# The ramp of a graph attention stage reordered

## The reference

```
h   = layernorm(x)                                  # [N, 256]
s1  = (h @ W[:256]) @ a_w ;  s2 = (h @ W[256:]) @ a_w
e   = s1[:, None] + s2[None, :] + a_b
e   = where(e >= 0, e, 0.2 * e) ;  e = where(adj > 0, e, -9e15)
x   = x + softmax(e, axis=1) @ (h @ fc_w + fc_b)
```

## Time and profile before

| | |
|---|---|
| median of the runs | 1169.57 us |
| profiled execution, its span | 1167.08 us, 1165.3 us |
| TensorE busy | 1032.5 us, 89% |
| VectorE busy | 757.0 us, 65% |
| ScalarE busy | 618.3 us, 53% |
| mean granted TensorE clock | 0.949 |
| first product of the ramp | 16.32 us |
| first exponential | 67.09 us |

### The profile page before, as it was taken

How to read it: one execution, slowest core, us unless ns; L and a number is a source line. 1 busy time by engine, 2 the same in 40 slices (tenths; PEclk the granted TensorE clock), 3 DMA queues, 4 the chain that set the end, 5 groups by cost and what they waited for, 6 DMA issues and landing times. The chain is left out here.

```text
span 1165.3 us, 23845 instructions
## 1 busy us (share of the span) xinstructions
PE 1032.5 (89%) x7616; PEld 823.2 (71%) x7617; DVE 757.0 (65%) x1598; ACT 618.3 (53%) x948; POOL 446.8 (38%) x363
## 2 busy tenths in 40 slices
PE   6639999999999599898987999996499999999991
PEld 5538989898989589687754888885266666666661
DVE  3799999999992464855675566666355455454550
ACT  1677888888873577767642112221145454454441
POOL 0244666666662000019140134453134444444443
PEclk9969999999999599899999999998699999999996
DMA  9998777777710311220053799998323333333322
GB/s 379 191 299 270 228 248 230 245 229 244 235 50 1 112 73 63 83 73 1 1 118 81 187 246 225 256 245 298 117 46 46 54 51 48 54 46 54 51 40 23
DMA packets 72587, 161.49 MB, mean 139 GB/s; under 512 B 7504, under 2 KB 58448, under 8 KB 66512
## 3 DMA queue, kind: packets, MB, share of 16 engines
q1 hardware_dynamic: 48656, 97.59, 26.9%
q0 software_dynamic: 18128, 40.17, 19.6%
q10 hardware_dynamic: 5744, 22.94, 5.5%
HBM read 137.34 MB, written 45.49 MB: 157 GB/s over the span
## 5 line engine op out<-in xcount | busy, mean ns | idle before, releaser
L554 PE MATMUL PS<-G,PT 128*128 128x256 f16 x2028 | 233.6, 273 | 0.0
L554 PEld LDWEIGHTS PS<-G,PT 128*128 128x128 f16 x2028 | 198.4, 98 | 22.1
L1576 PE MATMUL PS<-W,X 128*128 x708 | 165.5, 384 | 8.6 <-DVE X L1732 6.6
L1576 PEld LDWEIGHTS PS<-W,X 128*128 128x128 f16 x708 | 69.5, 98 | 97.0 <-issue 31.7
L1502 PE MATMUL PS<-own_H,adj_room 128*128 128x256 f16 x572 | 129.3, 272 | 0.0
L1500 PE MATMUL PS<-own_H,adj_room 128*128 128x257 f16 x572 | 129.3, 273 | 0.0
L1822 POOL DMA_INDIRECT out_dram<-X,place_i x59 | 92.2, 1563 | 88.4 <-DVE place_i L1746 80.6
L420 DVE SCALAR_TENSOR_TENSOR score<-S2low,S1low,S2row 128x3327 f32<-128x3327 f32 x26 | 114.5, 4405 | 1.4 <-ACT S2low L299 1.4
L538 PE MATMUL PS<-ident,probs 128*128 128x128 f32 x676 | 90.5, 280 | 26.0 <-ACT probs L327 16.8
L1596 PE MATMUL PS<-adj_room,X 128*128 x472 | 111.6, 380 | 0.3 <-issue 0.3
L426 DVE CUSTOM_DVE_ANT_0 score<-score,maskbias 128x3327 f32<-128x3327 f32 x26 | 100.0, 3848 | 6.2 <-DVE score L420 6.0
(11 more groups left out here) (273 smaller groups left out, 1991.8 us busy)
## 6 DMA issues: line engine op xcount, KB each, us to landing
adjf<-adj_dram SPq DMA_DIRECT2D x26, 1664.0 KB, 8.0
slot_rows<-blank SPq DMA_DIRECT2D x26, 1032.0 KB, 10.9
adj_room<-adjT_dram POOLq DMA_DIRECT2D x22, 832.0 KB, 9.8
W<-eW_dram ACTq DMA_DIRECT2D x8, 1024.0 KB, 4.8
adj_room<-eW_dram ACTq DMA_DIRECT2D x8, 1024.0 KB, 9.1
X<-slot_rows SPq DMA_DIRECT2D x59, 129.0 KB, 3.3
own_H<-eb_dram SPq DMA_DIRECT2D x8, 512.0 KB, 5.2
adj_room<-eW_dram ACTq DMA_DIRECT2D x8, 512.0 KB, 7.5
```

The lines of the kernel that those rows point to most:

```text
L554: mm = nc.tensor.matmul(acc[u][:, 0:D], left, right, start=(j == 0 and n == 0), stop=(j == T - 1 and n == 2))
L1576: mm = nc.tensor.matmul(psHE[u][:, n * F1:(n + 1) * F1], left[u][:, k, :], W1[:, e, k, part, n * F1:(n + 1) * F1], start=(m == 0), stop=(m ...
```

## The change

- **u on VectorE.** W is loaded as it stands (four blocks of 128 rows by 256), aw as a row that all 128 partitions hold. Four multiply-and-sum operations give uw [128, 4]. fcw moves from ScalarE's queue to the head of SP's.
- **Centring beside it.** The column sums of fcw and of u are made apart, by TensorE from fcw and from uw directly; the copies into fcwx are gone, and VectorE writes the centred result there. All of this stands ahead of row_moments(0) now.
- **Moments one group ahead.** row_moments(1) and gains(0) come before group 0; gains(n+1) and row_moments(n+2) stand inside group n, after the G_lo of its first pair. ScalarE's deviation(n+1) comes ahead of group n's G_hi.
- **Row copies two tiles earlier, mask of tile 0 earlier.** row_back(c) stands after G_hi(4c+5), not G_hi(4c+7); no_edge(0) stands ahead of the G_hi of the last group.
- **First score row in two parts.** leaky and masked of tile 0 for columns 0 to 2559 stand before the last four G_lo, those for the rest after them; a maximum of two joins them.

```diff
-        WT = score[1][:, 0:KD * 2 * D].rearrange("p (k n) -> p k n", k=KD)
+        W = score[1][:, 0:2 * KD * D].rearrange("p (k n) -> p k n", k=2 * KD)
...
         @block.sync
+            sp.dma_start(fcw[:, :, :], dram["fcw"].rearrange("(k p) n -> p k n", p=P)).then_inc(fcw_in, 16)
...
         @block.scalar
-            act.dma_start(WT[:, :, :], dram["WT"].rearrange("(k p) n -> p k n", p=P)).then_inc(u_in, 16)
-            act.dma_start(aw[:, :], dram["aw"]).then_inc(u_in, 16)
-            act.dma_start(fcw[:, :, :], dram["fcw"].rearrange("(k p) n -> p k n", p=P)).then_inc(fcw_in, 16)
+            act.dma_start(aw, dram["aw"]).then_inc(u_in, 16)
+            act.dma_start(W[:, :, :], dram["W"].rearrange("(k p) n -> p k n", p=P)).then_inc(u_in, 16)
...
-            deviation(0)
             act.wait_ge(fcw_in, 16)
             nc.scalar.activation(probs[0][:, 0:KD * D], fcw[:, :, :].rearrange("p k d -> p (k d)"), ACT.Square,
                                  accum_out=fsq[:, :]).then_inc(f_squared, 1)
+            deviation(0)
...
             for n, (a, b) in enumerate(XG):
-                if n > 0:
-                    deviation(n)
-                if n == len(XG) - 1:
+                if n + 1 < len(XG):
+                    deviation(n + 1)
+                else:
                     nc.scalar.activation(spent[:, :], big[:, :], ACT.Exp, scale=-1.0).then_inc(exp_waits, 1)
+                    no_edge(0, 0)
                 for i in range(a, b):
                     G_hi(i)
-                    if i % 4 == 3 and i >= 7:
-                        row_back((i - 7) // 4)
-            for c in range((T - 8) // 4 + 1, len(CK)):
-                row_back(c)
-            no_edge(0, 0)
+                    if i % 4 == 1 and i >= 5:
+                        row_back((i - 5) // 4)
+            row_back(len(CK) - 1)
             no_edge(1, 1)
...
         @block.vector
+            def leaky_part(n, a, b):
+                dve.wait_ge(s_low, 1)
+                dve.wait_ge(row_copied, 2 * -(-b // (4 * P)))
+                v.scalar_tensor_tensor(score[0][:, a:b], S2low[:, a:b], S1low[:, 0:1], S2row[:, a:b], ALU.add,
+                                       ALU.max).then_inc(leaky_part_done, 1)
+
+            def masked_part(n, a, b):
+                dve.wait_ge(mask_ready, 1)
+                dve.wait_ge(leaky_part_done, n + 1)
+                v.tensor_tensor_reduce(score[0][:, a:b], score[0][:, a:b], bias[0][:, a:b], 1.0, -2 * FAR,
+                                       ALU.subtract, ALU.max, part_max[:, n:n + 1]).then_inc(parts_done, 1)
...
+            dve.wait_ge(u_in, 32)
+            for m in range(2 * KD):
+                v.tensor_tensor_reduce(uj[m], W[:, m, :], aw, 1.0, 0.0, ALU.mult, ALU.add, uw[:, m:m + 1]).then_inc(u_done, 1)
+            dve.wait_ge(fcw_in, 16)
+            dve.wait_ge(mean_done, 1)
+            for k in range(KD):
+                v.scalar_tensor_tensor(fcwx[:, k, 0:D], psM[:, 0:D], -1.0 / D, fcw[:, k, :], ALU.mult,
+                                       ALU.add).then_inc(centred, 1)
+            dve.wait_ge(u_summed, 1)
+            v.tensor_scalar(u_mean[:, :], psU[:, 0:2], -1.0 / D, None, ALU.mult).then_inc(u_added, 1)
+            dve.wait_ge(u_added, 1)
+            for k in range(KD):
+                v.tensor_tensor(fcwx[:, k, D:D + 2], uw[:, k:k + 3:2], u_mean[:, :], ALU.add).then_inc(centred, 1)
             row_moments(0)
...
+            row_moments(1)
+            gains(0)
+            early = CK[-2][0] * P
             for n, (a, b) in enumerate(XG):
-                if n > 0:
-                    row_moments(n)
-                gains(n)
                 row_scores(a // 2)
                 for q in range(a // 2, b // 2):
                     if 2 * q + 2 < b:
                         row_scores(q + 1)
+                    if 2 * q + 4 == T:
+                        leaky_part(0, 0, early)
+                        masked_part(0, 0, early)
                     G_lo(2 * q)
                     G_lo(2 * q + 1)
+                    if 2 * q == a:
+                        if n == 0:
+                            dve.wait_ge(s_ready, 2)
+                            v.tensor_scalar(S1low[:, 0:4], S12[:, 0:4, 0], ALPHA - 1.0, None, ALU.mult).then_inc(s_low, 1)
+                        if n + 1 < len(XG):
+                            gains(n + 1)
+                        if n + 2 < len(XG):
+                            row_moments(n + 2)
...
-            leaky(0, 0)
-            masked(0, 0)
+            leaky_part(1, early, N)
+            masked_part(1, early, N)
+            dve.wait_ge(parts_done, 2)
+            v.tensor_tensor(rowmax[0][:, :], part_max[:, 0:1], part_max[:, 1:2], ALU.max).then_inc(masked_ready, 1)
             leaky(1, 1)
             masked(1, 1)
...
         @block.tensor
-            pe.wait_ge(u_in, 32)
-            for m in range(2 * KD):
-                for k in range(KD):
-                    mm = nc.tensor.matmul(psU[:, m:m + 1], WT[:, k, m * P:(m + 1) * P], aw[:, k:k + 1],
-                                          start=(k == 0), stop=(k == KD - 1))
-            mm.then_inc(u_done, 1)
             pe.wait_ge(unit_set, 1)
+            pe.wait_ge(fcw_in, 16)
+            for k in range(KD):
+                mm = nc.tensor.matmul(psM[:, 0:D], unit[:, :], fcw[:, k, :], start=(k == 0), stop=(k == KD - 1))
+            mm.then_inc(mean_done, 1)
+            pe.wait_ge(u_done, 2 * KD)
+            for k in range(KD):
+                mm = nc.tensor.matmul(psU[:, 0:2], unit[:, :], uw[:, k:k + 3:2], start=(k == 0), stop=(k == KD - 1))
+            mm.then_inc(u_summed, 1)
             pe.wait_ge(f_squared, 1)
```

More of the change, by code:

```diff
@@ L164, in attention @@
         xT = PT[:, :, :].rearrange("p q n -> p (q n)").bitcast(F32).rearrange("p (t k n) -> p t k n", t=T, k=KD)
-        WT = score[1][:, 0:KD * 2 * D].rearrange("p (k n) -> p k n", k=KD)
-        fcw = score[1][:, KD * 2 * D:KD * 3 * D].rearrange("p (k n) -> p k n", k=KD)
+        W = score[1][:, 0:2 * KD * D].rearrange("p (k n) -> p k n", k=2 * KD)
+        fcw = score[1][:, 2 * KD * D:3 * KD * D].rearrange("p (k n) -> p k n", k=KD)
+        aw = score[1][:, 3 * KD * D:3 * KD * D + D]
+        uj = [score[1][:, (3 * KD + 1 + m) * D:(3 * KD + 2 + m) * D] for m in range(2 * KD)]
         raw = sb("raw", [P, 8 * P])
@@ L169, in attention @@
         unit = raw[:, 8 * P - P:8 * P]
-        aw = sb("aw", [P, KD])
+        uw, u_mean = sb("uw", [P, 2 * KD]), sb("u_mean", [P, 2])
         ab, ab_low = sb("ab", [P, 1]), sb("ab_low", [P, 1])
@@ L176, in attention @@
         S1low = sb("S1low", [P, T])
-        big, spent = sb("big", [P, 1]), sb("spent", [P, 1])
+        big, spent, part_max = sb("big", [P, 1]), sb("spent", [P, 1]), sb("part_max", [P, 2])
         small = lambda n: [sb(f"{n}{u}", [P, 1]) for u in range(2)]
@@ L462, in iteration @@
                     leaky(t + 3, 1 - u)
-            row_moments(0)
-            dve.wait_ge(fcw_in, 16)
-            for k in range(KD):
-                v.tensor_copy(fcwx[:, k, 0:D], fcw[:, k, :]).then_inc(u_copied, 1)
-            dve.wait_ge(u_done, 1)
-            for k in range(KD):
-                v.tensor_copy(fcwx[:, k, D:D + 2], psU[:, k:k + 3:2]).then_inc(u_copied, 1)
+            dve.wait_ge(u_in, 32)
[11 more added lines that the diff above has]
+                v.tensor_tensor(fcwx[:, k, D:D + 2], uw[:, k:k + 3:2], u_mean[:, :], ALU.add).then_inc(centred, 1)
+            row_moments(0)
             dve.wait_ge(f_rooted, 1)
@@ L477, in _ @@
             v.tensor_scalar(g_scale[:, :], frecip[:, :], FULL / ROW_BOUND, None, ALU.mult).then_inc(f_chain, 1)
-            dve.wait_ge(mean_done, 1)
-            for k in range(KD):
-                v.scalar_tensor_tensor(fcwx[:, k, :], psM[:, 0:D + 2], -1.0 / D, fcwx[:, k, :], ALU.mult,
-                                       ALU.add).then_inc(centred, 1)
             dve.wait_ge(ab_in, 16)
@@ L574, in iteration @@
                     products(t - 1, 1 - u, 3)
-            pe.wait_ge(u_in, 32)
-            for m in range(2 * KD):
-                for k in range(KD):
-                    mm = nc.tensor.matmul(psU[:, m:m + 1], WT[:, k, m * P:(m + 1) * P], aw[:, k:k + 1],
-                                          start=(k == 0), stop=(k == KD - 1))
-            mm.then_inc(u_done, 1)
-            pe.wait_ge(unit_set, 1)
+            pe.wait_ge(unit_set, 1)
+            pe.wait_ge(fcw_in, 16)
[6 more added lines that the diff above has]
+            mm.then_inc(u_summed, 1)
             pe.wait_ge(f_squared, 1)
             nc.tensor.matmul(psR[0][:, 0:1], unit[:, :], fsq[:, :], start=True, stop=True).then_inc(f_summed, 1)
-            pe.wait_ge(u_copied, 2 * KD)
-            for k in range(KD):
-                mm = nc.tensor.matmul(psM[:, 0:D + 2], unit[:, :], fcwx[:, k, :], start=(k == 0), stop=(k == KD - 1))
-            mm.then_inc(mean_done, 1)
             pe.wait_ge(ident_in, 16)
-            pe.wait_ge(centred, KD)
```

(5 more changed lines are left out.)

11 lines of the change are left out of this document (6 added, 5 removed).

## The result

The changed kernel took 1164.91 us, the median of seven runs between 1163.17 and 1166.14. The kernel before, run beside it, took 1171.04 (seven runs, 1167.49 to 1175.29). The ratio is 0.9952, with a 95% interval of 0.9935 to 0.997: 5.6 us faster, between 3.5 and 7.6. The time is inside the predicted range, but at its fast end, and what happened is the rival in which W comes early, not the forecast: the first sum on VectorE started at 8.6 us, not at 10.3. The profiled execution took 1166.08 us (span 1164.3, mean granted clock 0.95).

What follows compares the result with a forecast made beforehand. TensorE and VectorE are full in the loop, so only the ramp's length counts: 13.0 less W's landing 10.3 less clock 0.9 gives 1.8 us, 1169.57 to 1167.8 us; 8-in-10 range 1164.0 to 1172.5.

Steps and rivals of the forecast that it cites:

- the rival in which W comes early: Load queues: W lands under 9.5 us, gain 3.5 to 5.7, time 1164 to 1166 us; chance 0.23.
- the forecast: Ramp: w 9.5 to 13 with a clock price of 0 to 1.8, time 1166 to 1171 us; chance 0.50.
- W's landing: Load queues: ScalarE's and SP's packets alternate, W's 512 rows gain 190 beyond their turn, landed at 10.3 us; ends 7.3 and 15.
- The even share of bytes: Load queues: turns by whole packets of descriptors give W at 7.3 us, gain 5.7; chance 0.07, within early W's 0.23.
- From W to the end of the first row: Ramp from W's landing to the end of tile 0's first mask-and-max: 50.3 us, against 51.2 from fcw's landing before.
- w: Start of the ramp: the moment W and aw have landed, taken as 10.3 us.
- The clock: TensorE in the ramp: a stall may bring 1.2 GHz, costing 1.8 us; half taken, 0.9 us.
- The reordering itself is thus worth 0.9 us.: Ramp behind the landing: three us won in the tail, about as many lost to mask(0), two stalls replace three; 0.9 us.
- The loop: Attention loop behind the ramp: untouched, PE and DVE full, so all of the earlier start is passed on.
- Strict alternation: Load queues: w = 13.5 to 15, loss 0.5 to 2, with the clock up to 3.8, 1170 to 1173.4 us; chance 0.14.
- TensorE at 1.2 GHz through the middle: Ramp: clock low from w + 20 to w + 30, 4.7 us lost beyond the sum, 1171.5 to 1176 us; chance 0.08.
- the change does nothing: Loop: an earlier start is taken up later by tile 2's mask or adjacency loads, 1169.6 us; chance 0.05.

Runs made afterwards that it cites:

- wide rows: Kernel after with W and fcw stored so that a partition's share is one row (128 of 4 KB, 128 of 2 KB): 1157.25 us, ratio 0.9941.
- order only: Start of the kernel before, everything from the first product on reordered as in the change: 1165.26 us, ratio 1.0002 to the kernel before.
- start only: New start of the change (sums on VectorE, centring, queues) with the old order behind it: 1160.0 us, ratio 0.9956 to the kernel before.
- moments between: Kernel after with moments, gains and deviation back between the groups: 1170.58 us, one run; also with wide rows and mask behind a row copy: 1160.83 us.
- Mask last: Kernel after with the mask of tile 0 put back behind ScalarE's last row copy: 1162.8 us, one run.
- W late: Kernel after with W's load moved from ScalarE's queue to SP's, behind X of group 1: 1175.96 us, one run.
- all: Kernel after with wide rows, mask of tile 0 behind the copy after G_hi(21), and moments of groups 2 and 3 later: 1155.78 us, ratio 0.9888.

## Why the prediction was right in its steps and off in its size

The predicted shift of the first exponential was 1.8 us, and it was 4.97. So what held was the range, which reached down to an early W, and not the sum: its three misses all went the same way, and none cancelled another. The terms, one by one:

- **W's landing: the step that was mis-sized.** Taken: 10.3. Measured: 8.61, 1.7 us of the 3.2 missed. The packets in each microsecond, of which five lines stand here, say how:

```profile
q10 hardware_dynamic: 121, 0.11, 42.1%
...
q10 hardware_dynamic: 196, 0.20, 57.0%
...
q1 hardware_dynamic: 162, 0.19, 54.2%
...
q1 hardware_dynamic: 82, 0.34, 86.3%
q10 hardware_dynamic: 84, 0.06, 18.9%
```

The first is the window 2 to 3 us, the next two 3 to 4, the last two 7 to 8 (packets, MB, share of the 16 engines; q10 is ScalarE's queue, q1 SP's). ScalarE's queue had 143 packets out by 3 us, where the prediction, from the earlier trace rows, let it begin in 3 to 4. Up to 7 us it had sent 638 against SP's 508. So it went 130 beyond its turn, and not the 190 taken: that part was guessed too large, not too small. What made W early, as these rows are read, is the earlier beginning, and that the packets it took turns with were short ones, fcw's 1 KB rows above all: 1.2 KB on average in 3 to 4 us. The mechanism, a turn for a turn by rows, stands: 82 to 84 packets in 7 to 8 us, 64 to 62 in 8 to 9, and the wide rows. Equal counts alone could also come of turns of several rows each. The packets' times in the kernel before decide it. From 8 to 12 us, with 249 packets of SP's queue and 250 of ScalarE's, there are 298 pairs in which a packet of ScalarE's starts 1 to 6 ns ahead of the end of one of SP's, and 300 the other way round, but only 66 and 64 pairs within one queue, no more than by chance: the next packet is the other queue's. Why ScalarE's queue begins earlier when it begins with aw, and why it goes beyond its turn, was not tried.
- **The even share of bytes.** The prediction names the Trainium skill, DMA: Bandwidth & Descriptors, "Queues, rings and completion order", for turns by whole packets of typically 9 to 17 descriptors, and draws from it an even share of bytes and a landing at 7.3. The page states the turns; the even share does not follow from them, since turns of equally many rows leave the small rows the smaller share too. The trace shows turns of one row, so it does not agree with the page's turns either, and no even share of bytes: 0.34 to 0.06 MB in 7 to 8 us. With ScalarE's queue as the change has it W came at 8.61 to 9.52 in eight executions, and as 128 rows of 4 KB at 6.89 to 7.41 in three.
- **From W to the end of the first row.** Predicted w + 50.3, measured 58.29, that is w + 49.7, with 0.6 of slowed products in it; without them w + 49.1, 1.2 us less than predicted. The sums took 0.35 each, not 0.40, and products started at w + 3.1, not 3.5; row scores at w + 9.2, not 10; project(6) at w + 21.9, not 23.3. Each term was a little large, none was wrong in kind. Of the 3.2 us missed this is 1.2.
- **The clock.** Taken: 0.9, half of one slowed group. Measured: 0.6, the last 0.3 of the miss. In the other executions with the three stalls it was between 0.6 and 3.3, and no run of this order had none. The prediction's choice lay within, its bound of 1.8 was too low: two stalls can both cost.
- **"The reordering itself is thus worth 0.9 us."** This was a sum of two things, and the split was not drawn. The start takes 3.1 us from landing to first product, not 4.25, which is 1.15 for it. Measured, the whole is 51.2 - 49.7 = 1.5: 1.15 from the start, 1.1 because one execution had 1.7 of slowed groups and the other 0.6, and -0.7 from the order. So the order itself loses a little; order only measured 1.0002, with a later first exponential. Of its parts, the moments still paid for by queued G_lo and the stall behind the mask are there. The three microseconds won in the tail are not: from the last project to the first exponential, slowed time off, it is 17.2 us before, 17.4 in start only and 15.8 in after and in order only, so 1.4 to 1.6 are won, while 1.9 to 2.5 are lost between the first product and the last project. The mask's place is what loses them. Path is 52.9 with the mask ahead of G_hi(18) and 49.9 with it behind the copy, with moments between 53.4 and 50.4, and 51.9 in start only. Mask last showed only that the early mask costs ahead of the last project what it saves behind it.
- **The loop.** Passed on one to one: it lasted 314.5 to 315.0 us in every one of the fourteen profiles, for first exponentials between 55.70 and 70.23.
- **The rivals.** W early happened, with gains of 3.5 to 5.7 predicted and 5.0 seen in the marks. Strict alternation is what W late imitates: by its marks 3.1 us are lost, where the rival said 0.5 to 3.8. TensorE at 1.2 GHz through the middle did not happen in any run: at most two groups in a row were slowed. Its price was also summed wrongly: six products at 3.5 in place of 1.97 make 9.2 us, not 4.7; the ten microseconds at half speed that it names make about 5. That the change does nothing is excluded by the ratio.

What stays open: why the stretch between the loop and the experts, with the same code, varies by 9.5 us over the profiles, and by up to 6.8 on one chip. The granted clock doesn't explain it: in 640 to 800 us the kernel after had 0.91 in two windows and before had 1.00 in all, but in 540 to 600 us it is the other way round. One window of before and one of after:

```profile
540.00:560.00 20.00, 17.25 (x131) 13.79 (x132) 12.20 (x28) 11.77 (x21) 15.06 (x17) 0.91 0.01 2
...
700.00:720.00 20.00, 18.69 (x158) 15.96 (x157) 11.31 (x59) 4.08 (x6) 8.96 (x10) 0.91 0.96 217
```

## What to carry to other kernels

When everything behind a point keeps its order, cost the landing that opens it first, in rows of each queue and not in bytes: here 1.2 to 2.6 us came from storing a matrix so that a partition reads one row. An operation pulled ahead in an in-order queue is free only where the queue has time: the same mask was worth nothing at two places and three microseconds at a third, and the same moments gave 0.5 or 2.2. A change of several parts is to be split at once into its start and its order; one gave all, the other nothing.

## What the runs showed of the hardware

- **Two full queues take turns row by row.** Whatever a row held, the queues of SP and ScalarE moved one each: 64 to 64 in 9 to 10 us of the kernel before, with 5.6 and 1.1 KB on average, 82 to 84 and 64 to 62 in 7 to 9 us of the kernel after. In the first microseconds of a transfer ScalarE's queue went beyond its turn (158 to 34 in 4 to 5 us of the kernel before).
- **Stalls of two microseconds can bring the low clock.** Groups of eight products took up to 3.7 us in place of 2.0 behind single stalls of 2.05, 2.62 and 3.17 us. The same stalls brought nothing elsewhere: 2.05 at 30.46 in the kernel after. From project(3) on, over all fourteen profiles, some of the group was slowed behind 6 of the 14 single stalls of 1.8 to 2.7 us, behind all eight of 2.8 or more, and behind all five pairs of stalls of 0.8 to 1.3 and 1.0 us with 0.43 us of transposes between, as in start only at 33.10. Behind none of the nine stalls of 1.0 to 1.4 with at most 0.5 ahead of the transposes, nor behind the pair of 0.59 and 0.98 at 24.29 in the kernel *all*, was one slowed. The kernel after and its repeat differ although the code is the same, so what decides it between these stays open. A slowed group costs up to 1.7 us where TensorE is on the path and nothing where a later wait swallows it.
- **A tiny GpSimd operation beside a long one of VectorE.** The shift, 128x1, took 3.42 us at 58.58, while leaky(1) ran on VectorE from 58.27 to 61.95. It is on the path: the first exponential waits for it. It took 3.36 in the kernel before at the same place, and 3.46 beside leaky(2) at 65.95. At 73.36, with VectorE at its work from PSUM (line 446), it took 0.19:

```profile
73.09 1.22 DVE L446 TENSOR_TENSOR PT<-PS,PT 128x1024 f16<-128x1024 f32 x1
...
73.36 0.19 POOL L255 TENSOR_SCALAR shift_by<-rowmax 128x1 f32<-128x1 f32 x1 [3.95 <-DVE rowmax L440]
```

That VectorE's work is what holds the shift is read from these times; no run changed it. Making the shift elsewhere was not tried.
